# Two loads and a bias moved in the first expert stage, and half a norm, half a gate and one stage slot moved in the second attention

## The reference

```
xn = layernorm(x)
s  = 16 heads mixed before and after a top-8 softmax, 16 memory keys, causal
g  = silu(top-2 of 8 experts, hidden silu(h1 * h3) of 256, then @ Wf + bf)
x  = x + s * g
xn = layernorm(x)
h  = layernorm(xn) * norm_w + norm_b           # the second norm inside layer two
q, k, v = h @ qkv_w.T + qkv_b ;  w = softmax(q^T k over channels) ;  s = (w v) @ proj_w.T + proj_b + xn
g  = silu(top-2 of 8 experts with capacity 80, relu hidden of 512)
x  = x + s * g
```

## Time and profile before

| | us |
|---|---|
| median of 3 runs | 1499.78 |
| the profiled execution | 1501.54 |
| its span | 1499.8 |
| PE busy | 1372.5 (92%) |
| DVE busy | 1099.2 (73%) |
| POOL busy | 891.1 (59%) |
| ACT busy | 805.8 (54%) |
| first experts, from the first `up0` to the last `down0` | 244.5 to 376.4 |
| tail, from the last `down` | 1430.6 to 1499.8 |

### The profile page before, as it was taken

One profiled execution on the slowest core, in us unless ns is written; L12 is line 12 of the kernel. 1 busy time (PEld: TensorE's weight loads), 2 busy tenths in 40 slices (PEclk: granted clock), 3 DMA queues, 4 the chain that ended last, 5 costly groups with the idle time before them and its releaser, 6 DMA issues.

```text
span 1499.8 us, 32740 instructions
## 1 busy us (share of the span) xinstructions
PE 1372.5 (92%) x10049; PEld 1196.4 (80%) x10049; DVE 1099.2 (73%) x3639; ACT 805.8 (54%) x1737; POOL 891.1 (59%) x1766
## 2 busy tenths in 40 slices
PE   5999998899789899999999999999999999899964
PEld 5548997777688789889988988998898889788842
DVE  7727884676588788878878887886888788554765
ACT  3546664444355556566665665665666566432321
POOL 5247784667666746655574674656567576723552
PEclk9999999999899999999999999999999999999997
DMA  7026001322500000000000000000000000012221
GB/s 246 13 81 205 23 24 55 106 78 57 169 16 9 18 12 10 9 13 16 8 18 12 11 9 11 18 7 17 12 10 12 2 26 7 10 48 72 70 80 42
DMA packets 70109, 62.27 MB, mean 42 GB/s; under 512 B 10809, under 2 KB 58020, under 8 KB 69939
## 3 DMA queue, kind: packets, MB, share of 16 engines
q1 hardware_dynamic: 61746, 44.96, 9.9%
q0 software_dynamic: 8192, 15.23, 3.5%
HBM read 32.88 MB, written 25.17 MB: 39 GB/s over the span
## 4 chain that ended last, share of the span: by engine, by line
PE 58%; DVE 14%; issue 10%; POOL 9%; POOLq 3%; ACT 2%; DMA 2%; DVEq 1%; SPq 0%; ACTq 0%
PE sa L1867 12%; PE sc L1845 11%; PE mb L1874 10%; PE tr L1856 7%; PE sc L1711 4%; DVE kept L1405 3%; POOL attn L797 3%; DVE top L1395 3%; PE mb L2081 2%; POOL x_slots L766 2%; PE sc L1847 2%; POOLq L698 1%; PE sa L1911 1%; POOL attn_mem L802 1%; PE tr L1716 1%
## 5 line engine op out<-in xcount | busy, mean ns | idle before, releaser
L797 POOL TENSOR_SCALAR attn<-kept,rden 128x128 f32<-128x128 f32 (+3 forms) x512 | 290.1, 567 | 345.1 <-DVE rden L1409 295.5
L1395 DVE MAX8 top<-sc 128x8 f32<-128x144 f32 (+3 forms) x512 | 263.0, 514 | 154.9 <-PE sc L1847 153.8
L1845 PE MATMUL sc<-k_hl,x_hl 128*128 128x272 f32 (+3 forms) x1920 | 373.7, 314 | 3.1 <-issue 3.1
L1867 PE MATMUL sa<-wv,attnT 128*128 128x128 f32 x2560 | 371.2, 276 | 0.0
L1038 ACT ACTIVATE attnT<-tr 128x128 f32<-128x128 f32 (+3 forms) x512 | 223.6, 437 | 269.5 <-PE tr L1856 258.1
L1032 ACT ACTIVATE ex<-sc,nmax 128x144 f32<-128x144 f32 (+3 forms) x512 | 277.1, 541 | 103.2 <-DVE nmax L1397 96.7
L1867 PEld LDWEIGHTS sa<-wv,attnT 128*128 128x128 f32 x2560 | 326.7, 192 | 6.3 <-issue 6.1
L1845 PEld LDWEIGHTS sc<-k_hl,x_hl 128*128 128x128 f32 x1920 | 284.1, 192 | 22.7 <-issue 12.3
L1405 DVE SCALAR_TENSOR_TENSOR kept<-sc,top,ex 128x144 f32<-128x144 f32 (+3 forms) x512 | 289.3, 565 | 1.5 <-issue 1.1
L1856 PE MATMUL tr<-ident,attn 128*128 128x128 f32 x1280 | 230.9, 278 | 41.2 <-POOL attn L797 39.0
L1856 PEld LDWEIGHTS tr<-ident,attn 128*128 128x128 f32 x1280 | 139.1, 142 | 54.3 <-POOL attn L797 50.2
(11 more groups left out here) (330 smaller groups left out, 2013.2 us busy)
## 6 DMA issues: line engine op xcount, KB each, us to landing
x_slots<-sg SPq DMA_DIRECT2D x1, 4608.0 KB, 17.1
y_pick<-x_slots SPq DMA_DIRECT2D x18, 256.0 KB, 3.2
y_slots<-wv SPq DMA_DIRECT2D x18, 256.0 KB, 2.4
x_slots<-sg SPq DMA_DIRECT2D x1, 2560.0 KB, 18.1
fb<-L_ffn_b SPq DMA_DIRECT2D x2, 1024.0 KB, 10.3
arena<-L_attn_x SPq DMA_DIRECT2D x8, 256.0 KB, 3.2
fb<-L_ffn_W SPq DMA_DIRECT2D x8, 256.0 KB, 6.1
fb<-x_slots SPq DMA_DIRECT2D x16, 128.0 KB, 2.4
```

The costliest lines, as they stand in the source:

```text
L797: pool.tensor_scalar(dst, src[:, NM:NM + P * (t + 1)], rden[:, t:t + 1], 1.0, ALU.mult, ALU.mult).then_inc(attn_ready.sem, 1)
L1395: dve.max(top8[:, t, :], src).then_inc(top_done.sem, 1)
L1845: pe.matmul(dst[:, lo:hi], x_hl[:, a, t * P:(t + 1) * P], k_hl[:, m, k, lo:hi], start=(i == 0), stop=(i == 2 and hi < w), skip_group_check ...
L1867: ins = pe.matmul(sa[:, t * C:(t + 1) * C], src[:, j * P:(j + 1) * P], wv[:, j, k, :], start=False, stop=False, skip_group_check=True)
```

## The change

In the **first experts**:

- `xg0` has four buffers instead of two (the new ones in `attn`, free once row 0 is through), so the load of group q waits for the turning of group q - 4 instead of q - 2; the store of a group is queued on SP behind the load of the group seven later, instead of four.
- `y0_out` on ACT and `y0_bias` on POOL go. A `y0_bias` on DVE reads PSUM and adds the bias in one pass, four instructions of 128x128 a group.
- PE and DVE read the two experts of a duo ahead: right behind the duo before, both at once.
- `x_turned(1)`, `x_highs(1)` and `x_lows(1)`, the split of row 1's input, stand at d = 36, ahead of the last three `down0`, instead of behind them.
- `keys(1, 0, 0)` uses the unsplit weights `mt_all` in one matmul in place of three with split ones; PE waits for the last y0 group behind it. POOL puts `next_g(0, 0)` ahead of `split_m`.

In the **second attention**:

- `hnorm` moves from DVE to ACT (scale and bias of an ACTIVATE; the bias, minus mean times rstd, is one DVE instruction for all rows).
- Of `take_z` the four multiplications (`half_z`) move to ACT; DVE keeps the four that multiply and add.
- A unit takes 3 slots instead of 4: slots 0 to 23 lie in the units, 24 to 69 in the tail.
- The tables name other slots for picks and gates.

```
-            for q in range(GROUPS0):
-                if q >= 2:
-                    sp.wait_ge(xg0_turned, q - 1)
-                sp.dma_start(xg0[q % 2], x0_slots[q * T:(q + 1) * T].rearrange(...)
+            for q in range(GROUPS0):
+                if q == 2:
+                    sp.wait_ge(tr_ready.sem, tr_ready.at(1, 0))
                 if q >= 4:
-                    store_y0(q - 4)
+                    sp.wait_ge(xg0_turned, q - 3)
+                sp.dma_start(xg0[q % 4], x0_slots[q * T:(q + 1) * T].rearrange(...)
+                if q >= 7:
+                    store_y0(q - 7)
...
+            def y0_bias(q):                                   # DVE
+                dve.wait_ge(y0_ps, 2 * q + 2)
+                if q >= 2:
+                    dve.wait_ge(y0_stored[q % 2], 16 * (q // 2))
+                for j, e in enumerate(experts_of.pop(2 * q) + experts_of.pop(2 * q + 1)):
+                    ins = dve.tensor_tensor(y0_sb[q % 2][:, j * C:(j + 1) * C], mbs[q % 2][:, j * C:(j + 1) * C],
+                                            b2f_b[:, bass.ds(e, 1), :].rearrange("p o c -> p (o c)"), ALU.add)
+                ins.then_inc(y0_ready, 1)
...
-            for d in range(DUOS0 + 1):                        # DVE
+            for d in range(DUOS0 + 3):
                 if d < DUOS0:
                     hidden0(d)
-                if d:
+                if d + 1 < DUOS0:
+                    load_experts(d + 1)
+                if 1 <= d <= DUOS0:
                     silu0(d - 1)
                 if d % 2 == 0 and d // 2 + 1 < GROUPS0:
                     low0(d // 2 + 1)
+                if d == DUOS0:
+                    x_lows(1)
+                if d >= 4 and d % 2 == 0:
+                    y0_bias(d // 2 - 2)
...
             def keys(b, it, k, guard):                        # PE
-                if b == 0:
+                if b == 0 or (b == 1 and it == 0):
                     return misc(b, it, f"keys{k}", guard, [(0, T, mt_all[:, it, k, :], xnT[:, :], True, True)])
...
+            def hnorm(r):                                     # ACT
+                if r >= 2:
+                    act.wait_ge(hT_ps.sem, r - 1)
+                for t in range(NT):
+                    ins = act.activation(hn[r % 2][:, t, :], xn_all[:, r, t * C:(t + 1) * C], ACT.Identity,
+                                         bias=nbias1[:, r, t:t + 1], scale=rstd1[:, r, t:t + 1])
+                ins.then_inc(hn_ready.sem, 1)
+
+            def half_z(r):                                    # ACT
+                act.wait_ge(taken[r % 3].sem, 16 * PICKS * (r // 3 + 1))
+                if r >= 2:
+                    act.wait_ge(out_ready.sem, r - 1)
+                for t in range(NT):
+                    ins = act.activation(z[r % 2][:, t * C:(t + 1) * C], y_pick[r % 3][:, 0, t, :], ACT.Copy,
+                                         scale=p_pick[:, r, t:t + 1])
+                ins.then_inc(z_half.sem, 1)
...
-        TAKE_Z = {16: 0, 24: 1, 32: 2, 36: 3, 44: 4, 52: 5, 60: 6, SLOTS_C: 7}
-        GATES = {18: 0, 26: 1, 34: 2, 38: 3, 46: 4, 54: 5, 62: 6, SLOTS_C + 1: 7}
+        TAKE_Z = {13: 0, 19: 1, 25: 2, 31: 3, 44: 4, 53: 5, 61: 6, SLOTS_C: 7}
+        GATES = {16: 0, 22: 1, 30: 2, 38: 3, 47: 4, 55: 5, 63: 6, SLOTS_C + 1: 7}
...
-                slot = 4 * (n - E1)
+                slot = 3 * (n - E1)
```

More of the change, by code:

```diff
@@ L226, in build @@
         tile_f = memT[0:1, 128:128 + TILES0]
-        xg0 = [y0_pick[:, i, :, :] for i in range(2)]
+        xg0 = [y0_pick[:, i, :, :] for i in range(2)] + [attn[:, i * T:(i + 1) * T].rearrange("p (s c) -> p s c", c=C) for i in range(2)]
         x0T_hl = [[x_hl[:, i, :] for i in range(2)], [k_hl[:, i, 0, 0:T] for i in range(2)]]
@@ L320, in build @@
         scattered0 = sem("scattered0")
-        xg0_loaded = [sem("xg0_loaded0"), sem("xg0_loaded1")]
+        xg0_loaded = [sem(f"xg0_loaded{i}") for i in range(4)]
         xg0_turned = sem("xg0_turned")
@@ L399, in build @@
         hn_ready = sig0("hn_ready")
+        nbias1_ready = sem("nbias1_ready")
+        z_half = sig0("z_half")
         hT_ps = sig0("hT_ps")
@@ L1210, in _ @@
                     act.activation(xn_all[:, B - 1, :], flat(xn1), ACT.Copy).then_inc(xn1_kept.sem, 16)
-            for i in range(4 * E1, SLOTS_C):
+                if n == E1 - 1:
+                    act.wait_ge(nbias1_ready, 1)
+                    act.wait_ge(xn1_kept.sem, xn1_kept.at(B, 0))
+                    hnorm(0)
+            for i in range(3 * E1, SLOTS_C):
                 evacuate_c(i)
+            half_z(B - 1)
             tanh_z(B - 1)
@@ L1362, in low0, with load_experts @@
                 dve.tensor_tensor(x0T_hl[q % 2][1], tr[:, :], x0T_hl[q % 2][0], ALU.subtract).then_inc(x0T_low, 1)
+            experts_of = {}
+            def load_experts(d):
+                experts_of[d] = [dve.value_load(tile_e[0:1, 2 * d + j:2 * d + j + 1], min_val=0, max_val=E0 - 1) for j in range(2)]
             def hidden0(d):
@@ L1367, in hidden0 @@
                     dve.wait_ge(hu0_ready, d - 1)
-                for j in range(2):
-                    e = dve.value_load(tile_e[0:1, 2 * d + j:2 * d + j + 1], min_val=0, max_val=E0 - 1)
+                for j, e in enumerate(experts_of[d]):
                     ins = dve.tensor_tensor(hb0[d % 2][:, j, :], bank(2 * (d % 2) + j),
@@ L1609, in take_z @@
                 dve.wait_ge(taken[r % 3].sem, 16 * PICKS * (r // 3 + 1))
-                for t in range(NT):
-                    dve.tensor_scalar(z[r % 2][:, t * C:(t + 1) * C], got[:, 0, t, :], p_pick[:, r, t:t + 1], None, ALU.mult)
-                dve.drain()
+                dve.wait_ge(z_half.sem, r + 1)
                 for t in range(NT):
@@ L1645, in evacuate_c @@
                     dve.tensor_tensor(xn_all[:, r, :], c_bank(i), xn_all[:, r, :], ALU.add).then_inc(s1_ready.sem, 1)
-                if i % 8 == 5 and i // 8 + 1 < B:
-                    hnorm(i // 8 + 1)
                 if name == "v":
@@ L1689, in _ @@
                     y_of(n - 1)
-                if n >= E1:
-                    evacuate_c(slot + 3)
                 if n == E1 - 1:
-                    dve.wait_ge(xn1_kept.sem, xn1_kept.at(B, 0))
-                    hnorm(0)
+                    dve.wait_ge(rstd1_ready.sem, rstd1_ready.at(B, 0))
+                    dve.scalar_tensor_tensor(out=nbias1[:, :, :], in0=mv1[:, :, :, 0], scalar=-1.0, in1=rstd1[:, :, :],
+                                             op0=ALU.mult, op1=ALU.mult).then_inc(nbias1_ready, 1)
             y_of(UNITS_E - 1)
-            for i in range(4 * E1, SLOTS_C):
+            for i in range(3 * E1, SLOTS_C):
                 evacuate_c(i)
```

86 lines of the change are left out of this document (35 added, 51 removed).

## The result

The changed kernel takes 1480.79 us in the median of 4 runs (1477.33 to 1482.57), the kernel before 1497.94 in 4 (1495.31 to 1501.0): ratio 0.9882, 95% interval 0.9852 to 0.9912. The forecast was 1481 from 1499.78, a ratio of 0.9877. The profiled execution of after is the fastest of its four, 1477.33 with a span of 1475.6.

What follows compares the result with a forecast made beforehand. PE was taken as pace setter, not full in the first experts and tail but full in the units. From 1499.78 us, -10.3 - 1.0 - 6.1 - 2.5 + 1.5 = -18.4 gave 1481 us; 8-in-10 range 1470 to 1494.

Steps and rivals of the forecast that it cites:

- The term of 3.15 us for a duo: First experts: PE would need 3.15 us per duo, 36 of them 113.4 us instead of 123.7, saving 10.3 us.
- PE's 2.90: First experts: PE's mean time per duo where neither issue nor token waits occur, a floor of 104.4 us for 36.
- 0.25 for bare reads: First experts: 0.25 us per duo for expert reads not fully hidden behind six matmuls; bounds were 0 and 0.72.
- The drain behind the last up: End of the first experts: it loses one read on DVE and a POOL wait, -1.0 us.
- DVE sets the pace: Rival, first experts: DVE needs 3.44 us a duo, so the 10.3 us saving goes; 1492 us, chance 0.17.
- 1.14 in the sum: First experts: the y0 bias costs DVE 1.14 us a group, 0.57 us per duo.
- DVE's own 2.97 a duo: First experts: DVE's instructions take 2.97 us per duo, some 3.1 with the gaps between them.
- The paired reads stand bare: slower: Rival, first experts: two reads in a row stay unhidden, a duo takes 3.8 to 4.1 us; 1505 to 1515 us, chance 0.09.
- the four buffers: First experts: loads issued three groups ahead remove PE's 9.0 us of waits for gathered tokens.
- The hole: Between the first experts' last down and row 1's first score: 8.66 us shrinks to 2.5, -6.1 us.
- The clock: Start of row 1: the 6.4 us at 0.50 of the clock should mostly not come, -2.5 us, bounds 0 and -3.2.
- Units and tail: Second attention: units save 5.8 us, the tail holds one more row; together +1.5 us, bounds -6 and +8.

Runs made afterwards that it cites:

- the doubled bias: The changed kernel with the y0 bias of every group done twice on DVE, with a drain between: 1494.79 us, ratio 0.9987 to the kernel before.

## Why the prediction was right, and where it was not

**The first experts.** The term of 3.15 us for a duo was met (6.36 / 2 = 3.18 in the steady part; the 36 ups take 110.8 us where 113.4 were forecast), but its reason was wrong. I built it as PE's 2.90 plus 0.25 for bare reads. The chain through DVE is the pace setter, as the doubled bias shows, and where DVE does not hold it PE takes 5.88 / 2 = 2.94 a duo, 0.04 for its reads. Moved on both engines, the reads are worth 0.6 us of the stage (119.46 with them back, 118.85 without), not 16 or 7: the 5 us that PE gains are lost on DVE, whose odd bias, freed of its reads, ends before the tanh is ready, so that the product starts ahead of the silu (292.67 against 293.17). The drain behind the last up lost 0.3 us and not 1.0. My rival "DVE sets the pace" had the mechanism and the wrong price, 3.44 a duo: the y0 bias took 0.87 us a group, where I had 1.14 in the sum and 1.8 in the rival; DVE's own 2.97 a duo left out the 0.58 us of waiting and the 0.65 by which a silu is held in each group. "The paired reads stand bare: slower" is excluded by the run with the reads between: with both in either place the stage differs by 0.6 us.

By subtraction of stages the 13.1 us are: 131.94 - 130.90 = 1.0 clock; 130.90 - 123.37 = 7.5 the four buffers (forecast 9.0, which I had read as PE's wait for tokens); 123.37 - 119.46 = 3.9 the y0 bias that left ScalarE and GpSimd (forecast nothing of its own; the early split of row 1's input is in it, with 0.1 at most); 0.6 the reads. Each is a difference of single traces; the last three terms are between stages that all began at full clock. That the sum came out so near (-18.4 forecast, -17.2 between the medians) is luck: PE's gain and DVE's loss by the reads and the worth of the moved y0 bias were each mis-sized, and the errors cancel.

**What I had not seen is the hold between DVE and GpSimd.** The silu has both of its large inputs in SBUF, and so has the product. Where the silu starts first it takes 0.68 us and the product 1.66; where the product starts first it takes 1.29, and the silu 1.33, ending 0.54 after the product. In the run with the low part ahead and DVE's reads between its biases the silu of 298.31 takes 1.40 and ends 0.55 after the product of 297.88. The biases, with one input in PSUM, run beside the product at their usual 1.27 to 1.29 for two. The rows for it stood in the trace of before (products of 1.65 and of 1.27, silus of 0.68 and of 0.90 to 1.25 in one stage), and I took the short silu. Two of them, a silu behind a product:

```profile
312.08 1.28 POOL L879 TENSOR_TENSOR ht<-h 128x512 f32<-128x512 f32 x1 [0.20 <-DVE h L1370]
312.66 1.25 DVE L1376 SCALAR_TENSOR_TENSOR hh<-hh,ht 128x512 f32<-128x512 f32 x1 [0.66 <-ACT hh L993]
```

The Trainium skill (SBUF — State Buffer, SBUF: two separate sides) says that a DVE operation with two SBUF inputs and a GpSimd operation that reads SBUF exclude each other, whoever starts first keeping the ports for the whole instruction; the trace agrees, for the second comer takes longer by about what is left of the first (silu 0.65 longer with 0.79 left, product 0.37 longer with 0.53 left).

With PE's issue beside it, this fact goes far in sorting the orders of the first experts: none held, PE's reads ahead 5.88 us a group; none held, PE's reads between 6.3; one of two held by 0.65 with DVE's reads hidden 6.36; one held by 0.5 and DVE waiting for PE's up 6.36; one held by 0.7 in the path to PE 7.13. It does not sort them all: with the y0 bias ahead of the odd silu hardly any silu is held, and a group still takes 6.36. What closes the chain there was not tried, and no run takes the hold away by itself.

The Trainium skill (DMA: Bandwidth & Descriptors, Latency and other measured facts) has a floor of about 600 ns for a tensor_load; by it six matmuls would hide two. Behind six matmuls PE's turning waited 0.3 us a time for issue in after (2.7 in 9) and 0.45 with the low part ahead (7.2 in 16), so two reads are mostly but not wholly hidden; the floor itself no run here measured.

**The hole.** 8.66 to 2.55 us, as forecast (2.5). 2.8 of it came from POOL, which lost the y0 bias and was reordered (8.66 to 5.89 with turning and keys as before), 3.3 from the early turning and the unsplit keys. The clock gave 1.65, not 2.5: the 6.40 us that PE filled at half clock in before hold only 5.12 us of its work at full clock in after, and the row waits on other engines between (PE busy 79.00 of 85.28 us in before).

**Units and tail.** Net +1.0 for units 8 to 15 and the tail against +1.5, and 1.0012 with this part alone. The five rows took 61.3 us where 63.15 were forecast, the units gave 5.3 and not 5.8, and the first cwT came 1.5 us behind the last down, not 0.7. The norm on ScalarE took 1.64 us in place of 1.3 and hid. A slot costs 0.66 to 0.84 us in the units (5.3 and 6.7 for eight) and 1.7 behind them (13.5 for eight); so taking eight out of the units was the loss that the lighter DVE paid for. The prediction had both prices and did not draw that conclusion; the run with four slots did. That the gate behind the maximum is what shortened a tail row was not tried alone.
